# Attention scores by query: the third row of blocks of four heads in one group of two ordered halves, five groups a unit in place of six

## The reference, cut to what matters

```
qkv = jnp.einsum('bsm,qhkm->qbhsk', x, w_qkv)
scores = jnp.einsum('bhsk,bhtk->bhst', Q, K) / jnp.sqrt(d_k)
scores = jnp.where(causal, scores, -jnp.inf)
probs = jax.nn.softmax(scores, axis=-1)
attn = jnp.einsum('bhst,bhtk->bhsk', probs, V)
```

## Time and profile before

| what | us |
|---|---|
| median of three runs | 1568.94 (1568.85 to 1570.51) |
| profiled execution, its own time | 1567.27 |
| its span | 1565.5 |
| first maximum of the attention (L1917) to last join (L1930) | 1236.95 to 1484.0 |
| the same point of two successive sequences | 31.01 apart in the steady part |

### The profile page before, as it was taken

One profiled execution on the slowest core, in us unless ns is written; L12 is line 12 of the kernel. 1 busy time (PEld: TensorE's weight loads), 2 busy tenths in 40 slices (PEclk: granted clock), 3 DMA queues, 4 the chain that ended last, 5 costly groups with the idle time before them and its releaser, 6 DMA issues. The chain is left out here.

```text
span 1565.5 us, 44459 instructions
## 1 busy us (share of the span) xinstructions
PE 1515.0 (97%) x16156; PEld 918.7 (59%) x16156; DVE 1253.5 (80%) x2574; ACT 933.7 (60%) x1826; POOL 893.2 (57%) x940
## 2 busy tenths in 40 slices
PE   7999999999999999899999999999998899999998
PEld 4666666666666666666666666666663444444443
DVE  7976777767887799886777777778779989999968
ACT  7755555555555444365555555556653378888853
POOL 2855756657664255455756657657447434444455
PEclk9999999999999999999999999999999989999999
DMA  4300000000001244200000000000011212111112
GB/s 165 106 12 5 7 0 7 7 0 7 1 8 35 35 87 84 43 5 5 8 1 7 7 0 7 3 4 9 3 15 26 51 36 63 36 43 43 29 32 71
DMA packets 75264, 43.50 MB, mean 28 GB/s; under 512 B 54858, under 2 KB 71786, under 8 KB 74996
## 3 DMA queue, kind: packets, MB, share of 16 engines
q1 hardware_dynamic: 75124, 41.64, 11.5%
HBM read 10.51 MB, written 2.10 MB: 8 GB/s over the span
## 5 line engine op out<-in xcount | busy, mean ns | idle before, releaser
L662 POOL TENSOR_TENSOR scratch<-scratch 128x512 f16<-128x512 f32 x379 | 441.5, 1166 | 381.6 <-ACT scratch L900 381.3
L1470 DVE SCALAR_TENSOR_TENSOR scratch<-psum,scratch 128x512 f32<-128x512 f32 x512 | 352.5, 689 | 235.7 <-PE psum L2067 213.3
L895 ACT ACTIVATE scratch<-psum 128x512 f32<-128x512 f32 x512 | 305.2, 597 | 394.9 <-PE psum L2067 394.0
L2109 PE MATMUL psum<-ffn_down_hi,scratch 128*128 128x128 f16 x2048 | 369.3, 219 | 0.3
L2111 PE MATMUL psum<-ffn_down_hi,scratch 128*128 128x128 f16 x2048 | 369.3, 219 | 0.0
L2110 PE MATMUL psum<-ffn_down_lo,scratch 128*128 128x128 f16 x2048 | 369.3, 219 | 0.0
L900 ACT ACTIVATE scratch<-scratch 128x512 f16<-128x512 f32 x512 | 318.5, 622 | 12.1 <-DVE scratch L1470 11.9
L2109 PEld LDWEIGHTS psum<-ffn_down_hi,scratch 128*128 128x128 f16 x2048 | 200.3, 98 | 59.1 <-POOL scratch L662 0.7
L2110 PEld LDWEIGHTS psum<-ffn_down_lo,scratch 128*128 128x128 f16 x2048 | 200.3, 98 | 58.0
L2111 PEld LDWEIGHTS psum<-ffn_down_hi,scratch 128*128 128x128 f16 x2048 | 200.4, 98 | 0.0
L2065 PE MATMUL psum<-x_hi,ffn_up_hi 128*128 (+1 forms) x512 | 194.1, 379 | 2.0 <-DVE scratch L1470 2.0
(11 more groups left out here) (240 smaller groups left out, 2652.0 us busy)
## 6 DMA issues: line engine op xcount, KB each, us to landing
scratch<-scratch SPq DMA_DIRECT2D x96, 128.0 KB, 2.8
raw<-in_ffn_w_dram SPq DMA_DIRECT2D x8, 768.0 KB, 4.5
ffn_up_hi<-scratch SPq DMA_DIRECT2D x32, 128.0 KB, 2.7
x_tok<-in_x_dram SPq DMA_DIRECT2D x8, 256.0 KB, 7.3
out_dram<-x_tok SPq DMA_DIRECT2D x7, 256.0 KB, 2.0
raw<-in_lin_dram SPq DMA_DIRECT2D x1, 1092.0 KB
x_hi<-scratch SPq DMA_TRANSPOSE x46, 2.4
x_lo<-scratch SPq DMA_TRANSPOSE x46, 2.4
```

Of the source, the lines that this page charges most:

```text
L662: pool.tensor_tensor(h_lo[r], h32[r], h_hi[r], ALU.subtract).then_inc(s_plo, 1)
L895: act.activation(gate_act[k % 2], bank(k % 2), ACT.Silu, scale=W_DOWN).then_inc(s_s, 1)
L1470: dve.scalar_tensor_tensor(h32[k % HSLOTS], bank(5 + k % 2), W_DOWN, gate_act[k % 2], ALU.mult, ALU.mult).then_inc(s_h, 1)
L2109: pe.matmul(dst, h_hi[r][:, cols], hi, start=k % FC == 0 and n == 0, stop=False, skip_group_check=True)
```

## The change

Block row 2 of all four heads becomes one group, number 4, with 256 keys of two heads in each bank of its pair, and VectorE reads it with one reduction of 1024 elements. A unit has five groups instead of six; since five is odd, the pair of banks now goes by the running number of the group over all units. The first matmul into a bank marks the whole bank as fresh, so the two heads of a bank are written in two halves: `last_query(..., 0, ...)` writes heads 0 and 2 with `start`, and `last_query(..., 1, ...)` writes heads 1 and 3 behind a wait of TensorE for its own first half (new semaphore `s_p1half`). In the bodies the halves stand mostly where groups 4 and 5 stood with one tile by key between them; at A the second half comes ahead of three `weighted_values`, at B ahead of tile 7 and two `weighted_values`, at C ahead of `out_proj`. On VectorE the reduction of group 5 goes, so at A the join and then `q_low` and `k_low` follow the reduction of group 4, and at C the join and then `add`.

```
-        QT = 6
+        QT = 5
+        def query_banks(u, n):
+            return 2 * ((QT * u + n) % 2)
...
                     else:
-                        dve.tensor_reduce(heads[:, :, TWO], pair.rearrange("p (r o k) -> p r o k", r=2, o=1)[:, :, :, 0:2 * P], AX_X, ALU.max,
+                        dve.tensor_reduce(by(block_max[g % 2], HG)[:, :, TWO], pair.rearrange("p (r o k) -> p r o k", r=HG, o=1), AX_X, ALU.max,
                                           negate=True).then_inc(s_p1used, 1)
...
                     if more:
                         q_low(b + 1, 7)
                         k_low(b + 1, 4)
-                    maxima(u + 2, 2, 5)
                     maxima(u + 3, 3, 0)
...
+                def last_query(u, g, half, odd):
+                    at0 = query_banks(u, QT - 1)
+                    if half == 0:
+                        pe.wait_ge(s_p1used, QT * (u + 1))
+                    else:
+                        pe.wait_ge(s_p1half, u + 1)
+                    for x in range(2):
+                        rows, at = head(2 * x + half), 2 * half * P
+                        ins = pe.matmul(bank(at0 + x, at, at + 2 * P), q_stack[odd][g][rows, 2 * P:3 * P], k_stack[odd][g][rows, 0:2 * P],
+                                        start=half == 0, stop=half == 1, skip_group_check=True)
+                    ins.then_inc(s_p1 if half else s_p1half, 1)
...
-                    by_query(u + 2, 2, 4, odd)
+                    last_query(u + 2, 2, 0, odd)
                     pe.wait_ge(s_p2exp, KT * u + 10)
                     by_key(u, b, 0, 8, odd, 5)
+                    last_query(u + 2, 2, 1, odd)
                     if before:
                         weighted_values(u - 1, b - 1, 3, 1 - odd, 1)
                         weighted_values(u - 1, b - 1, 3, 1 - odd, 2)
                         weighted_values(u - 1, b - 1, 3, 1 - odd, 3)
-                    by_query(u + 2, 2, 5, odd)
                     by_query(u + 3, 3, 0, odd)
...
-                    by_query(u + 3, 3, 4, odd)
+                    last_query(u + 3, 3, 0, odd)
                     by_key(u + 1, b, 1, 6, odd, 4)
+                    last_query(u + 3, 3, 1, odd)
                     by_key(u + 1, b, 1, 7, odd, 5)
                     weighted_values(u, b, 0, odd, 2)
                     weighted_values(u, b, 0, odd, 3)
                     by_key(u + 1, b, 1, 8, odd, 7)
-                    by_query(u + 3, 3, 5, odd)
```

More of the change, by code:

```diff
@@ L459, in build @@
         UNITS = NB * NG
-        QT = 6
+        QT = 5
         OPENED = 4
         def query_tile(n):
-            return (2, 0)[n % 2], ([(i, i, 1, a * P) for a, i in enumerate((0, 2, 1, 3))], [(1, 0, 1, 0), (3, 0, 3, P)], [(2, 0, 2, 0)])[n // 2]
+            return (2, 0)[n % 2], ([(i, i, 1, a * P) for a, i in enumerate((0, 2, 1, 3))], [(1, 0, 1, 0), (3, 0, 3, P)])[n // 2]
+        def query_banks(u, n):
+            return 2 * ((QT * u + n) % 2)
         DIAGONAL, ONE_THREE, TWO = slice(0, SUB * SUB, SUB + 1), slice(11, 15), slice(4, 5)
@@ L1910, in maxima @@
                     dve.wait_ge(s_p1, QT * u + n + 1)
-                    r = query_tile(n)[0]
-                    pair = psum[:, 2 * (n % 2) * BANK:2 * (n % 2 + 1) * BANK]
-                    heads = by(block_max[g % 2], HG)[:, r:r + 2]
+                    at = query_banks(u, n)
+                    pair = psum[:, at * BANK:(at + 2) * BANK]
+                    if n < QT - 1:
+                        r = query_tile(n)[0]
+                        heads = by(block_max[g % 2], HG)[:, r:r + 2]
                     if n < 2:
@@ L2007, in body @@
                     if more:
-                        maxima(u + 4, 0, 5)
                         maxima(u + 5, 1, 0)
@@ L2545, in by_query @@
                 def by_query(u, g, n, odd):
-                    first, pieces = query_tile(n)
+                    at0 = query_banks(u, n)
                     if n == 0:
@@ L2550, in by_query @@
                     pe.wait_ge(s_p1used, QT * u + n + 1)
+                    first, pieces = query_tile(n)
                     for m, (i, k, w, at) in enumerate(pieces):
@@ L2553, in by_query @@
                             rows = head(first + x)
-                            ins = pe.matmul(bank(2 * (n % 2) + x, at, at + w * P), q_stack[odd][g][rows, i * P:(i + 1) * P],
+                            ins = pe.matmul(bank(at0 + x, at, at + w * P), q_stack[odd][g][rows, i * P:(i + 1) * P],
                                             k_stack[odd][g][rows, k * P:(k + w) * P], start=m == 0, stop=n > 1 and m == len(pieces) - 1,
@@ L2558, in by_query, with causal @@
                         ins.then_inc(s_p1, 1)
-                def causal(n):
-                    first = query_tile(n)[0]
+                def last_query(u, g, half, odd):
[9 more added lines that the diff above has]
+                    ins.then_inc(s_p1 if half else s_p1half, 1)
+                def causal(u, n):
+                    first, at0 = query_tile(n)[0], query_banks(u, n)
                     for i in range(HG):
@@ L2566, in causal @@
                             each_sub = causal_sb[rows, HG * P:HG * P + HR].rearrange("p (o k) -> p o k", o=1).to_broadcast([HR, SUB, HR])
-                            ins = pe.matmul(by(bank(2 * n + x), SUB)[:, :, i * HR:(i + 1) * HR], causal_sb[rows, i * P:(i + 1) * P], each_sub,
+                            ins = pe.matmul(by(bank(at0 + x), SUB)[:, :, i * HR:(i + 1) * HR], causal_sb[rows, i * P:(i + 1) * P], each_sub,
                                             start=False, stop=i == HG - 1, skip_group_check=True)
@@ L2619, in attention @@
                     by_query(0, 0, n, 0)
-                    causal(n)
+                    causal(0, n)
                 pe.wait_ge(s_epick, NS + 1)
-                for n in range(2, QT):
+                for n in range(2, QT - 1):
                     v_proj(0, 7, (n - 2,))
@@ L2625, in attention @@
                     by_query(0, 0, n, 0)
+                for half in range(2):
+                    v_proj(0, 7, (2 + half,))
+                    keep_warm(1, 6)
+                    last_query(0, 0, half, 0)
                 by_query(1, 1, 0, 0)
-                causal(0)
+                causal(1, 0)
                 max_rows(0, 0, 5)
                 by_query(1, 1, 1, 0)
-                causal(1)
+                causal(1, 1)
                 for n in range(2, 4):
@@ L2635, in attention @@
                 by_key(0, 0, 0, 1, 0, 4)
-                by_query(1, 1, 4, 0)
+                last_query(1, 1, 0, 0)
                 by_key(0, 0, 0, 2, 0, 5)
-                by_query(1, 1, 5, 0)
+                last_query(1, 1, 1, 0)
                 pe.wait_ge(s_p2exp, 4)
@@ L2656, in body @@
                     max_rows(u + 1, 1, 7)
-                    causal(1)
+                    causal(u + 2, 1)
                     if before:
@@ L2689, in body @@
                     by_key(u, b, 0, 9, odd, 7)
-                    causal(0)
+                    causal(u + 3, 0)
                     if more:
@@ L2775, in body @@
                     if more:
-                        by_query(u + 4, 0, 4, 1 - odd)
+                        last_query(u + 4, 0, 0, 1 - odd)
                     by_key(u + 2, b, 2, 10, odd, 5)
+                    if more:
+                        last_query(u + 4, 0, 1, 1 - odd)
                     if before:
```

23 lines of the change are left out of this document (10 added, 13 removed).

## The result

The changed kernel takes 1582.55 us (1580.49 to 1585.78), beside 1569.70 us of the kernel before on the same chips; the ratio is 1.0082, with a 95% interval of 1.0071 to 1.0093. It is slower by 12.9 us where 2.4 were forecast, and it lies outside the range. The profiled execution has a span of 1579.9 us and its own time is 1581.64.

What follows compares the result with a forecast made beforehand. VectorE was taken to set the pace, TensorE and ScalarE following with a little slack. +0.35 us a sequence times seven gave +2.4, the rest together 0: 1568.94 + 2.4 gives 1571.3 us, range 1565 to 1574.5.

Steps and rivals of the forecast that it cites:

- A: Place in a sequence where the first half follows the projections; `q_low` and `k_low` 1.16 us later, +0.33 to +0.6 us.
- B: Place in a sequence with the stall between groups 4 and 5; new wait covered because VectorE comes later, -0.28 us.
- C: Place in a sequence with the `add` behind the join; `add` loses its stall, next group's reduction earlier, -0.11 us.
- The reduction: On VectorE, one reduction of 1024 elements for two of 512; 0.08 us gained a unit, 0.30 a sequence.
- 64 matmuls of the halves: Sign of a right forecast: the matmuls of the halves stay unchanged in number, at 64.
- The two halves: TensorE's wait for its own first half: 0.32 us, bounds 0 and 0.4; group ready 0.64 us behind first issue.
- D: Place in a sequence where the first half stands behind 24 `weighted_values`; group ready later, +0.16 us net.
- Outside the steady part: Last body about -0.1 us, first two units -0.1, first body at granted clock 0.50 +0.2; together 0.
- rival 3: Granted clock at the attention's start: low stretch falls away, about 3.6 us less, or a second adds as much; chance 0.06.
- The covered halves: TensorE runs ahead at A, C and D, so the wait costs nothing; -5.3 us, 1563.6; chance 0.17.
- rival 2: Late low halves delay ScalarE's tile 9 and spread to C; +5 us, 1574; chance 0.23, including the forecast's chain above 1572.1.

Runs made afterwards that it cites:

- the experiment with the short reduction: Kernel before, with the reductions of groups 4 and 5 reading 128 instead of 256 keys a head; 1565.90 us, ratio 0.9966.
- the experiment with B alone: Changed kernel, with only the second half at B moved behind tile 7 and one `weighted_values`; 1581.59 us, ratio 1.0076.
- the second experiment: Kernel before, six groups, with the low halves of queries and keys moved behind group 5 and its join on VectorE; 1583.83 us, ratio 1.0081.

## Why the prediction was wrong, by its own steps

The main step that failed is the one at B: the prediction priced TensorE's wait for itself only where VectorE reads the merged group, and put it at nothing where VectorE comes later anyway. In the runs that wait costs 0.72 us a sequence and the later second half 0.50, where the whole sequence was forecast at +0.35.

**The reduction** was sized nearly rightly: the merged one takes 1.224 us, and by distance and stalls VectorE's work falls by about 0.2 a sequence (+1.39 of distance against +1.6 of stalls; 0.30 forecast). What it is worth was not: in the experiment with the short reduction VectorE's saved time counts at 43%. "VectorE sets the pace, and TensorE and ScalarE follow with a little slack" is the sentence that failed; that experiment shows that the chain through them is nearly as long. The sign "64 matmuls of the halves" was a miscount: four a unit are 128, and 128 they are in both kernels.

**The two halves.** I took 0.32 us from issue to consumer for a consumer that is TensorE. It is 0.35 at A and 0.43 at B, C and D, above the bound of 0.4 at three places, and the reduction starts 0.67 and 0.76 behind the first half instead of 0.64.

**A**: forecast a ready group 0.64 us behind the issue, `q_low` 2.1 us behind it; measured 0.67 and 2.13. The delay in the next unit was right too in kind: the join-to-join shares of A and B together grow by 0.16 (14.60 to 14.76), where I had +0.05 to +0.3.

**B** is the step that failed. "It is covered there" was true of VectorE and not of TensorE. VectorE gained its 0.28 there (the stall of 0.13 ahead of group 1 is the delay from A), but TensorE's queue stood 0.43 us behind the wait, and everything behind it with it: the transposed values, the transposed output, ScalarE's copy of it and VectorE's output copy in C. That is 0.49 of new stalls in C; the experiment with B alone shows the link. I had costed the wait only at the consumer, not at what is queued behind it on its own engine.

**C**: forecast -0.11. Its largest term, -0.26 for the stall of the `add`, did come. Against it stand the 0.49 from B, and 0.35 more ahead of the merged group (0.44 against 0.09), where 0.23 were forecast. A part of the saved time was waited away at D ahead of group 1 (0.17).

**D**: forecast +0.16, measured 0.54 more stall ahead of the group and 0.17 ahead of group 1. Beside the 0.24 forecast for the wait these are 0.12 of the longer way from issue to reduction, and 0.20 because the first half itself comes later behind VectorE's group 1 (3.27 us against 3.07).

Put together: +1.39 a sequence where +0.35 was forecast. By experiment 0.72 of it are TensorE's wait, 0.50 the second half's lateness without a wait, and 0.17 what is left.

**Outside the steady part** I had put nothing. Measured are +1.87 us up to the first join and +3.05 behind the last. Of the first, 0.75 are there when VectorE takes the first maximum of the attention (1237.70 instead of 1236.95), at the full clock. The rest comes at a lower one: in the changed kernel the stretch at 0.50 begins at 1238.7 instead of 1244.9 us, and the merged group of the first unit keeps VectorE waiting 1.08 us. Two further stretches of 3.4 us follow at 1262.6 and 1272.8, and behind the attention there is one of 6.8 us:

```profile
1484.00:1498.00 14.00, 12.53 (x160) 5.51 (x158) 12.12 (x19) 10.65 (x26) 4.30 (x7) 1.00 0.01 3
1498.00:1505.00 7.00, 7.00 (x59) 1.89 (x57) 2.51 (x13) 3.81 (x9) 4.52 (x8) 0.51 0.00 1
```

That is rival 3, a little above its 3.6 us; I gave it 0.06. That it belongs to the change is not settled: the mean granted clock differs between executions of one kernel (0.987 to 0.993 before, 0.985 to 0.991 changed). At an equal mean clock of 0.989, ten executions of the kernel before took 1570.3 to 1573.0 us and two of the changed one 1580.5 and 1581.6; at 0.991 the one of the changed kernel took 1580.5 and the twenty of the kernel before 1567.7 to 1573.1. So some 9 to 11 us are left without it, and seven times 1.39 is 9.7.

**The rivals.** The covered halves (faster) fell: TensorE had no lead at A, C and D, and VectorE stalled 0.44 to 0.62 us for the merged group at each. "Clearly slower" (rival 2) was the right side with the wrong mechanism: not the low halves, but the wait in TensorE's own queue. Its sign came true all the same: in the changed kernel ScalarE waits 0.51 us for tile 9 behind the low halves. With the low halves first that wait is gone and the distance is the same, so the sign could not tell the two apart.

Not tried: all four heads in the merged group without any order between its halves.

## What to carry to other kernels

A wait that an in-order engine makes for its own result can cost twice, as it did here: at the consumer, which gets the data late, and at everything that is queued behind it, even where the consumer has slack; follow the queue to the next engine that needs it. Merging two results into one read takes away the cover that the first one gave the second, so count the time from the first issue to the last write before you count the saved read. Before you read a cost per delay out of an experiment, look at the granted clock in each period of it: half of the loss in one experiment here was a stretch at 0.50. And an engine that is busy 96 to 97% of a steady part is not alone in setting the pace: take work off it in a run, and see what share of it comes back.

## What the runs showed of the hardware that was not expected

TensorE takes up again 0.35 us (A) or 0.43 us (B, C and D) after the issue of the matmuls of 256 columns that it waits for, while VectorE starts 0.32 to 0.33 us after the issue of such a pair. What makes the difference between A and the other places is left open.

The time from the last join to the end goes with the stretches at 0.50 in it: 81.8 to 82.4 us in the seven profiled executions without one (the last 3 us of the span left aside), 83.1 to 83.7 in four with 3.4 us, 84.3 to 84.8 in three with 6.8 us. A microsecond at the low clock costs 0.4 there, and the same in the steady part of the second experiment (1.5 us for a stretch of 3.4).

In the start of the attention VectorE and TensorE wait for each other, and the granted clock falls to 0.50 in every profile taken; three times as many idle-time matmuls behind each part of the projection went with 6.8 us less of it in the profiles of both kernels (20.5 to 13.7, and 27.3 to 20.5). What sets its begin is left open.
